# One packed program for three 16-wide attentions, with the clip attention's clamps on GpSimd

## What is computed

```
x = x + tanh(g_xattn[0]) * L0_xattn(layernorm(x), ctx)   # cosine similarity
x = x + tanh(g_ffn[0])   * L0_ffn(layernorm(x))
x = x + tanh(g_xattn[1]) * L1_xattn(layernorm(x), ctx, mask)
x = x + tanh(g_ffn[1])   * L1_ffn(layernorm(x))          # experts
x = x + tanh(g_xattn[2]) * L2_xattn(layernorm(x), ctx)
x = x + tanh(g_ffn[2])   * L2_ffn(layernorm(x))          # experts
x = x + tanh(g_xattn[3]) * L3_xattn(layernorm(x), ctx)
x = x + tanh(g_ffn[3])   * L3_ffn(layernorm(x))
```

```
q = query @ Wq + bq; k = key_value @ Wk + bk; v = key_value @ Wv + bv
attn = softmax(clip(q k^T * scale, -10000, 10000))
x = attn v @ Wo + bo
```

## Time and profile before

| | |
|---|---|
| median of 3 runs | 3416.39 us |
| the runs | 3400.31, 3416.39, 3434.22 us |
| span of the profiled execution | 3390.0 us |
| mean granted clock of TensorE | 0.829 of 2.4 GHz |
| busy: PE, DVE, ACT, POOL | 2575.8, 1580.7, 872.7, 785.2 us |

### The profile page before, as it was taken

One profiled execution on the slowest core, in us unless ns is written; L12 is line 12 of the kernel. 1 busy time (PEld: TensorE's weight loads), 2 busy tenths in 40 slices (PEclk: granted clock), 3 DMA queues, 4 the chain that ended last, 5 costly groups with the idle time before them and its releaser, 6 DMA issues.

```text
span 3390.0 us, 37402 instructions
## 1 busy us (share of the span) xinstructions
PE 2575.8 (76%) x13142; PEld 1918.9 (57%) x13142; DVE 1580.7 (47%) x2934; ACT 872.7 (26%) x2012; POOL 785.2 (23%) x709
## 2 busy tenths in 40 slices
PE   3795885487887728888888577673888884999998
PEld 3574554376666625555556466552555653766665
DVE  3443566256657423333334533224564554454454
ACT  1221342111111103323333112122453451232232
POOL 3103223334334133333434422213000000000000
PEclk8795676699898868888989588786896996988899
DMA  3704441122232230000000013321000000000000
GB/s 115 253 0 57 56 60 54 68 96 98 78 103 91 83 118 5 2 2 2 2 2 0 13 50 95 105 86 55 5 3 2 5 1 0 1 0 0 0 0 25
DMA packets 91147, 151.93 MB, mean 45 GB/s; under 512 B 7612, under 2 KB 75900, under 8 KB 88428
## 3 DMA queue, kind: packets, MB, share of 16 engines
q1 hardware_dynamic: 61820, 101.93, 11.1%
q0 software_dynamic: 8736, 27.76, 2.6%
q10 hardware_dynamic: 20496, 20.97, 1.7%
HBM read 90.51 MB, written 47.19 MB: 41 GB/s over the span
## 4 chain that ended last, share of the span: by engine, by line
PE 57%; issue 20%; DVE 10%; POOL 5%; DMA 3%; ACT 3%; SPq 1%; another core or an unknown queue 1%; ACTq 0%; DVEq 0%; POOLq 0%
PE bank L1898 11%; PE bank L1853 7%; PE bank L1736 6%; PE bank L1915 6%; PE bank L1737 5%; PE bank L1738 5%; PE bank L1939 4%; PE bank L1873 2%; DMA arena<-rows_by_expert 2%; POOL arena L786 2%; DVE nmax L1044 1%; PE bank L1987 1%; DVE split L1332 1%; PE bank L2091 1%; ACT arena L1457 1%
## 5 line engine op out<-in xcount | busy, mean ns | idle before, releaser
L1898 PE MATMUL bank<-arena 64*128 64x256 f32 x1536 | 472.4, 442 | 6.2 <-ACT arena L1457 6.2
L1898 PEld LDWEIGHTS bank<-arena 64*128 64x128 f32 x1536 | 283.0, 207 | 141.6 <-issue 108.5
L1542 ACT ACTIVATE arena<-bank,nmax 128x256 f32<-128x256 f32 x512 | 226.3, 470 | 459.8 <-DVE nmax L1044 457.8
L1915 PE MATMUL bank<-ident,arena 128*128 128x128 f32 x1536 | 272.0, 306 | 74.7 <-POOL arena L829 44.2
L1044 DVE TENSOR_REDUCE nmax<-bank 128x2 f32<-128x512 f32 x256 | 175.8, 690 | 321.0 <-PE bank L1898 316.9
L1457 ACT ACTIVATE arena<-bank 128x512 f32<-128x512 f32 (+1 forms) x346 | 198.2, 580 | 463.1 <-PE bank L1853 112.0
L1736 PE MATMUL bank<-split,ewl 128*128 128x512 f32 x514 | 227.3, 442 | 98.8 <-DVE arena L1329 86.2
L1915 PEld LDWEIGHTS bank<-ident,arena 128*128 128x128 f32 x1536 | 177.6, 151 | 210.1 <-issue 112.2
L700 POOL TENSOR_TENSOR rstd<-rstd,mhalf 128x2 f32<-128x2 f32 x40 | 28.0, 700 | 996.8 <-DVE rstd L972 839.2
L1329 DVE TENSOR_TENSOR arena<-sil,bank 128x512 f32<-128x512 f32 x136 | 93.2, 685 | 315.9 <-ACT sil L1670 300.3
L1737 PE MATMUL bank<-split,ewh 128*128 128x512 f32 x514 | 217.2, 423 | 0.0
(11 more groups left out here) (394 smaller groups left out, 4764.7 us busy)
## 6 DMA issues: line engine op xcount, KB each, us to landing
ew<-in_we SPq DMA_DIRECT2D x32, 768.0 KB, 8.0
ew<-in_we SPq DMA_DIRECT2D x15, 1408.0 KB, 6.1
rows_by_expert<-mrow ACTq DMA_DIRECT2D x1, 20480.0 KB, 58.2
arena<-rows_by_expert SPq DMA_DIRECT2D x23, 512.0 KB, 6.5
rows_by_expert<-arena SPq DMA_DIRECT2D x38, 256.0 KB, 5.4
...
```

The source lines that it names most:

```text
L1542: ins = A(prob[h % 3][:, t * S:(t + 1) * S], src[:, t * S:(t + 1) * S], ACT.Exp, bias=nmax[:, h, t:t + 1], **kw)
L1898: ins = mm(bank[h % 3][:, t * S:(t + 1) * S], q[r0:r0 + 64, gr, t * P:(t + 1) * P], kT[r0:r0 + 64, gr, :], start=True, stop=True)
L1915: ins = tr(bank[3 + k % 2][:, c0:c0 + P], prob[k % 3][:, t * S + kt * P:t * S + (kt + 1) * P], ident[:, :])
```

## The change

L3X and L3F leave the unpacked program and become instances of `Packed` with options: `bias`, `clip`, `proj` (an output product) and `own` (keys and values from x itself, masks by two more rows, registers). The functions `attention` keep L2X alone. All three run the same loops:

- Three rooms (banks 5, 6, 7) instead of two, and one bank for the values. x, queries, keys and values are made for image n+3 and not n+2. Projections are issued in halves, six matmuls at a time; DVE's two output blocks come at heads 5 and 7 and not together at head 8.
- The clip: DVE clamps the maxima (two small instructions) and shifts them by 60, so that exponentials reach at most e^60, and the exponentials are clamped to the range from e^-27 to e^60, in place, 128x512 per head. All 128 of these clamps go to POOL; `by_pool` says how many heads of the first h are POOL's, and DVE's own `clamp` is never issued. PE's `values` wait for the clamps.
- The output product: DVE writes the divided outputs to `on`, PE turns them, ACT copies them to `onT`, PE multiplies by the weights, DVE adds. The output bias times the gate (for L3X with the bias of the values folded in) is added to x by POOL beforehand (`with_bias`).
- For L3F, SP puts the mask rows into `qpack` and `kpack`, 8 DMAs per image; the registers have steps of their own (`register_scores`, `register_turned`, `register_values`, `registers`).
- `kpack` is filled with ones by POOL at the start of L1X and of L3X, where six DMAs did it; the weights of L3X and L3F are split by POOL in L2F.

```diff
+
+
+def by_pool(h):
+
+    return h
...
-        for n in range(-2, B + 1):
-            for what, at in (("xT", n + 2), ("k", n + 2), ("v", n + 2), ("m1", n), ("q", n + 2),
-                             ("z0", n - 1), ("z1", n - 1), ("m0", n + 1)):
-                if 0 <= at < B:
-                    b = sum(self.used) % 2
+        self.place, self.used = {}, [0] * ROOMS
+        for n in range(-3, B + 1):
+            for what, at, here in (("rs", n, own), ("m1", n, True), ("xT", n + 3, True), ("z0", n - 1, True),
+                                   ("rt", n, own), ("z1", n - 1, True), ("rg", n - 1, own), ("q", n + 3, True),
+                                   ("m0", n + 1, True), ("k", n + 3, True), ("ro", n, own), ("w", n - 1, proj),
+                                   ("v", n + 3, True), ("y", n - 1, proj)):
+                if here and 0 <= at < B:
...
+ROOMS = 3
+EXP_HIGH, EXP_LOW = 60.0, -27.0
 L1X = Packed("l1x", 0.25, mask=True)
-L2X = Attn("l2x", 64, 0.125, proj=True, bias=False)
-L3X = Attn("l3x", 16, 0.25, proj=True, bias=True, clip=True)
-L3F = Attn("l3f", 16, 0.25, proj=True, split=True)
+L2X = Attn("l2x", 64, 0.125)
+L3X = Packed("l3x", 0.25, bias=True, clip=True, proj=True)
+L3F = Packed("l3f", 0.25, proj=True, own=True)
 
...
+                for n in range(-3, B):
+                    ahead = 0 <= n + 2 < B
+                    if ahead:
+                        if n >= 1:
+                            sp.wait_ge(m["st"], at["st"] + n * NH)
+                        if n == -2:
+                            sp.wait_ge(m["ones"], at["ones"] + s.total["ones"])
+                            if s.own:
+                                sp.wait_ge(m["mc"], 1)
+                        sp.wait_ge(m["qs"], at["qs"] + 2 * n + 6)
+                        rows_of(qpack[(n + 2) % 3], qhl, 0, (0, 1, 0), m["pq"])
                     if 0 <= n:
...
+                    if not s.own and n + 4 < B:
+                        context(n + 4)
 
             if "l1x" in run:
...
+                def with_bias(n):
+                    pool.wait_ge(g["xn"], entered(s.name, n) * T + T)
+                    if n == 0:
+                        pool.wait_ge(m["bt"], at["bt"] + 1)
+                    rows = x[:, n * T:(n + 1) * T, :]
+                    nc.gpsimd.tensor_tensor(rows, rows, bot[:, :].rearrange("p (o d) -> p o d", o=1).broadcast_to([P, T, D]),
+                                            ALU.add).then_inc(m["xb"], 1)
+
+                def clamp(n, h):
+                    i = n * NH + h
+                    pool.wait_ge(m["e"], at["e"] + i + 1)
+                    w = pT16[i % 8][:, :]
+                    nc.gpsimd.tensor_scalar(w, w, math.exp(EXP_HIGH), math.exp(EXP_LOW), ALU.min, ALU.max)\
+                        .then_inc(m["cl"], 1)
+
...
+                    if ahead and not s.own:
                         context(n + 3)
-                    if n + 3 < B:
-                        root(m, n + 4, rstd[:, :], rstd[:, :], mhalf[:, 0:T])
+                    for h in range(NH):
+                        if s.clip and 0 <= n < B and by_pool(h + 1) > by_pool(h):
+                            clamp(n, h)
+                        if h == 4 and ahead:
+                            filled("xT", n + 3)
+                            parts(xT16, xt[:, :, :], "xs", n + 3)
+                        if h == 9 and ahead:
+                            filled("q", n + 3)
+                            if n + 3 > 0:
+                                pool.wait_ge(m["pq"], at["pq"] + s.loads * (n + 3))
+                            parts(qhl, qf[:, :, :], "qs", n + 3)
+                        if h == 10 and n + 4 < B and not s.own:
+                            root({"asked": asked[s.name]}, n + 5, rstd[:, :], rstd[:, :], mhalf[:, 0:T])
+                        if h == 12 and ahead:
+                            filled("k", n + 3)
+                            if n + 3 > 0:
+                                pool.wait_ge(m["pk"], at["pk"] + s.loads * (n + 3))
+                            parts(khl, kf[:, :, :], "ks", n + 3)
+                        if h == 13 and s.proj and n + 4 < B:
+                            with_bias(n + 4)
 
             def mixture(s):
                 m, r, at = mo, rooms[s.name], s.base
...
+                        ch.link(ts(nmf[:, c, :, :, :], nmf[:, c, :, :, :], -CLAMP / s.qscale, EXP_HIGH / s.qscale,
+                                   ALU.max, ALU.add))
+                        ch.link(ts(nmf[:, c, :, :, :], nmf[:, c, :, :, :], (CLAMP + EXP_LOW) / s.qscale, None, ALU.min))
                     for t in range(T):
...
+                def finish(n):
+                    src, done = made("y", n)
+                    dve.wait_ge(m["xb"], at["xb"] + n + 1)
+                    rows = x[:, n * T:(n + 1) * T, :]
+                    stt(rows, src[:, :].rearrange("p (t d) -> p t d", t=T), gate, rows, ALU.mult, ALU.add).then_inc(done, 1)
...
+                for n in range(-3, B + 2):
                     for h in range(NH):
+                        if h == 0 and s.proj and 0 <= n - 2 < B:
+                            finish(n - 2)
                         if 0 <= n + 1 < B:
                             maximum(n + 1, h)
                             if h == 7:
                                 maxima(n + 1, 0)
                             if h == NH - 1:
                                 maxima(n + 1, 1)
-                        if h == 4 and n + 2 < B:
...
+                        if h == 1 and s.own and 0 <= n < B:
+                            register_maximum(n)
+                        if h in (5, 7) and 0 <= n - 1 < B:
+                            outputs(n - 1, h // 2 - 2)
+                        if h == 8 and s.own and 0 <= n - 1 < B:
+                            with_registers(n - 1)
+                        if h == 9 and s.mask and 0 <= n + 3 < B:
+                            queries(n + 3)
+                        if h == 10 and n + 4 < B and not s.own:
+                            statistics(n + 4)
+                        if h == 12 and s.own and 0 <= n < B:
+                            register_outputs(n)
...
+                def projected(what, n, dst, used, bias):
+                    if n > 0:
+                        act.wait_ge(m[used], at[used] + 2 * n)
+                    src, done = made(what, n)
+                    if s.bias:
+                        for j in range(2):
+                            ins = A(dst[:, j, :], src[:, j * S:(j + 1) * S], ACT.Identity, bias=bias[:, j:j + 1])
...
-                                      lambda t: t[:, :].rearrange("p (t h e) -> p t h e", t=T, h=NH))
...
+                def across(what, n, j, w, of, r):
+                    b, k = s.place[what, n]
+                    if j == 0:
+                        room(what, n)
+                    to = bank[FIRST_ROOM + b]
+                    for c in range(DC):
+                        ins = mm3(to[:, j * S:(j + 1) * S], [t[0:r, c, j * P:(j + 1) * P] for t in w],
+                                  [of[:, u, c, :] for u in range(2)], c == 0, c == DC - 1)
+                    if j == 1:
...
-                    pe.wait_ge(m["e"], s.base["e"] + n * NH + gr * 4 + 4)
+                    pe.wait_ge(m["e"], at["e"] + n * NH + gr * 4 + 4)
+                    if s.clip:
+                        k = by_pool(gr * 4 + 4)
+                        pe.wait_ge(m["cl"], at["cl"] + n * by_pool(NH) + k)
+                        pe.wait_ge(m["cv"], at["cv"] + n * (NH - by_pool(NH)) + gr * 4 + 4 - k)
...
+                def finish(n):
+                    filled("w", n)
+                    to, done = room("y", n)
+                    for t in range(T):
+                        for c in range(DC):
+                            ins = mm(to[:, t * D:(t + 1) * D], onT[:, t * DC + c, :], wo[s.name][:, c, :],
+                                     start=c == 0, stop=c == DC - 1)
+                    ins.then_inc(done, 1)
...
+                for n in range(-3, B + 1):
+                    ahead = 0 <= n + 3 < B
+                    behind = 0 <= n - 1 < B
                     for h in range(NH):
                         heads_of(n, h)
-                        if h == 0 and n + 2 < B:
-                            turned(n + 2)
-                            keys(n + 2)
-                        if h == 1:
-                            if 0 <= n - 1:
-                                values(n - 1, 3)
-                            if n + 2 < B:
-                                values_of(n + 2)
+                        if h == 0 and s.own and 0 <= n < B:
+                            register_scores(n)
+                        if h == 1 and behind:
+                            values(n - 1, 3)
                         if h == 2 and 0 <= n < B:
                             maxima(n, 1)
-                        if h == 3 and n + 2 < B:
-                            queries(n + 2)
+                        if h == 3 and ahead:
+                            turned(n + 3)
```

(20 more changed lines are left out.)

1088 lines of the change are left out of this document (487 added, 601 removed).

## The result

The changed kernel takes 2841.5 us (median of 4 runs, 2833.8 to 2849.8), the one before 3424.3 in the runs beside it: a ratio of 0.832, 95% interval 0.827 to 0.838. That is 8.5 us under the low end of the range (2850), and 97 us under the forecast of 2939. The profiled execution took 2846.9 us, with a span of 2845.1.

The account below looks back on a forecast made before the run. The prediction took L3X and L3F to be bound by TensorE's work. Savings of 40.3 (L1X), 204.6 (L3X) and 232.7 us (L3F), 477.6 in all, took the span from 3390.0 to 2912.4 us, median 2939; range 2850 to 3060.

Parts of the forecast that it names:

- Where the gain comes from: Three 16-wide attentions: L1X 40.3 us less, L3X 204.6, L3F 232.7; other stages within 10 us of now.
- The length of an iteration: Full iterations with projections: 24 us in L1X (from 30.8), 26.5 in L3X, 29.5 in L3F, clock 0.75 to 0.8.
- rival (3): All three stages: TensorE gets the full clock nearly throughout and DVE binds; the low ends, 2843 us; chance 0.08.
- PE's work at the full clock: L1X's full iteration: PE's matmuls and transposes need some 25 us at half clock, some 13 at 2.4 GHz.
- the DVE bound of 20 us: L1X's iteration at full clock: DVE's 16 reductions, its other work and 40 handovers set the pace, 20 us.
- The tail of L1X: L1X's last images: two iterations without projections at 18.6 us each, the last at 13, then 7 of draining.
- cost nothing: L3X's clamps on POOL: value groups' wait just fits, costed at nothing; otherwise some 2 us per image.
- The four subtractions: L3X: DVE's four 8-column subtractions with two SBUF inputs may each wait for a clamp, 2.4 us per image.
- Filling, splits, SP: Filling 57.2, 60 and 55 us; weight splits in L2F cost nothing; SP's 24 DMAs per image, 16 us, hidden.
- The median as span plus 26: Whole kernel: the profiled span lay 26 us under the timed median, so 26 is added to the forecast span.
- All low ends together: Whole kernel: every stage at its low end, 573 us off the 3390 span, plus 26: 2843 us.
- half of a rival: Range's low end, 2850 us: half of the full-clock, DVE-bound case (2843 us, chance 0.08) left out.

Follow-up runs that it names:

- the repetition: The changed kernel run once more with nothing edited, beside a combined variant on the same chip: 2816.5 us, ratio 0.828.

## Why the prediction was right in its direction and too high by 97 us

**Where the gain comes from: right.** All but 7 of 545 us lie in the three stages, and the order of their shares is the one forecast. The other stages moved by 4 us at most.

**The length of an iteration: the step that failed.** "Evener work should cost the clock a little less often than 0.72; I take 24", and with it 26.5 and 29.5. Measured, the five iterations with projections of the three stages are 97.5, 116.5 and 116.5 us long, where 120, 132.5 and 147.5 were forecast: 69.5 us less. The three stages came in 60.7 under; the other terms gave 8.8 back. PE's granted clock was not 0.75 to 0.8: leaving out the first iteration of each stage, it was 1.00 in eleven of the other twelve with projections (0.76 in L3X's second). This was rival (3), which got 0.08; its time, 2843, was met within 2 us. That is luck twice over. Its span of 2817 us is 28 too short (its stages of 211, 232 and 236 us took 221.9, 249.8 and 241.0), and the 26 us that it adds for the median are 30 too long. And its reason was wrong. DVE, expected to be busy for 75% of the time and busy for 91, 85 and 71%, is not the bound at the full clock. In L3F PE is: busy for 23.78 of 23.80 us, and the run with doubled transposed scores shows it by lengthening one for one. For L1X (18.6 of 19.2 us) and L3X (21.0 of 22.3) the busy share says the same; no run tested it.

**PE's work at the full clock: too small.** I put it at some 13 us for L1X, half of 25, with 0.21 us for a pair of score matmuls at the half clock; it is 18.6. The pairs do run beside each other, but their price is that of a long row of them. The timeline of PE in L1X (start us, us, instruction) at 1.00, where two heads stand back to back, where a head stands between other work, and at 0.50:

```profile
416.44 0.28 PE L2037 MATMUL bank<-kpack,qpack 48*128 48x256 f32 x1
416.56 0.28 PE L2051 MATMUL bank<-qpack,kpack 50*128 50x256 f32 x1
...
418.00 0.38 PE L2037 MATMUL bank<-kpack,qpack 48*128 48x256 f32 x1 [0.18 <-DVE nmf L1117]
418.01 0.38 PE L2051 MATMUL bank<-qpack,kpack 50*128 50x256 f32 x1
418.23 0.28 PE L2037 MATMUL bank<-kpack,qpack 48*128 48x256 f32 x1
...
418.44 0.39 PE L2020 MATMUL bank<-ident,nmhl 128*16 128x128 f32 x2
...
435.71 0.58 PE L2037 MATMUL bank<-kpack,qpack 48*128 48x256 f32 x1
...
436.45 0.59 PE L2020 MATMUL bank<-ident,nmhl 128*16 128x128 f32 x2
```

Back to back, the next pair starts after 0.12 us. Between other work a head's two pairs hold PE for 0.44 us (418.00 to 418.44), and for 0.74 at the half clock (435.71 to 436.45). Sixteen heads at 0.44 are 7.0 us, where the sum had 3.5. The six matmuls of half a projection show the same pattern:

```profile
385.95 0.38 PE L1760 MATMUL bank<-xT,wqs 128*128 128x256 f32 x1
386.17 0.28 PE L1761 MATMUL bank<-xT,wqs 128*128 128x256 f32 x1
...
386.64 0.28 PE L1762 MATMUL bank<-xT,wqs 128*128 128x256 f32 x1
386.86 0.39 PE L2037 MATMUL bank<-kpack,qpack 48*128 48x256 f32 x1
```

The first and the last step of a group take 0.22 us, those between 0.12. So in these rows a group costs 0.12 us per matmul or pair and 0.20 more for standing between other work: 0.44 for two pairs, 0.92 for six matmuls. By the starts of its instructions the full iteration at 378.9 us then is 7.0 us of scores, 5.4 of projections (the sum had 3.9), 4.0 of value groups (as in the sum) and 2.4 of turning (1.5), 18.8 in all. The rows of before held a warning: if busy time goes with the clock, PE's 24.4 us at a mean of 0.72 make an estimated 17.6 us at the full clock (24.4 x 0.72), not 13.

So the DVE bound of 20 us that I took as the low end happened to lie near PE's real one, which is why rival (3) fits for another reason. And the 24 came from taking the waits away from L1X's old 30.8 at its old clock, so neither end of it was PE's own time.

**The tail of L1X: wrong the other way.** Forecast 18.6, 18.6, 13; measured 17.0, 22.2, 20.8. The last two images ran at 0.50 throughout, after an iteration in which PE was busy for only 13.5 of 17.0 us. It takes back 9.8 us and is not fixed: the same code had 17.8 and 15.3 in the repetition, after the same iteration (13.6 of 17.4 us busy). What decides between the two stays open.

**The clamps: price right, "cost nothing" wrong.** The clamp in L3X, forecast 0.61, with min, median and max in ns:

```profile
L765 POOL TENSOR_SCALAR pT<-pT x128: 606/614/648, 2337.1 to 2509.3; 128x512 f32<-128x512 f32 x128
```

No wait of PE names it, but with one column in place of 512 the stage is 13 to 22 us shorter. The forecast looked at the full iterations only, where it is 1.2 us, and not at those without projections, where it is 4. The placing itself was the best of the three tried: the Trainium skill (GPSIMD Engine Reference, 4.1 Engine selection) has elementwise work on VectorE, and here L3X with DVE's 0.49 us per clamp is 16 to 26 us longer than with POOL's 0.61. Without the clamps DVE is the fuller engine of the two.

**DVE beside the clamps.** The four subtractions were bounded with 2.4 us per image. In L3X DVE is busy 153.3 us, without the clamps 141.9: 1.4 us per image, 11.4 in all. Of these, 8.7 fall on three small instructions with both ends in SBUF: 6.5 on two that have one input (L1125 and L1127) and 2.2 on the subtractions (L1132). First with clamps, then without, DVE's groups by line:

```profile
L1125 DVE TENSOR_SCALAR nmf<-nmf 128x16 f32<-128x16 f32 x16 | 7.6, 473 | 0.6
L1127 DVE TENSOR_SCALAR nmf<-nmf 128x16 f32<-128x16 f32 x16 | 6.8, 427 | 0.5
L1132 DVE TENSOR_TENSOR nmhl<-nmf,nmhl 128x8 fp32r<-128x8 f32 x32 | 6.1, 232 | 0.5
```

```profile
L1125 DVE TENSOR_SCALAR nmf<-nmf 128x16 f32<-128x16 f32 x16 | 5.1, 322 | 0.5
L1132 DVE TENSOR_TENSOR nmhl<-nmf,nmhl 128x8 fp32r<-128x8 f32 x32 | 3.9, 164 | 0.6
L1127 DVE TENSOR_SCALAR nmf<-nmf 128x16 f32<-128x16 f32 x16 | 2.8, 174 | 0.6
```

The Trainium skill (SBUF — State Buffer, Who interferes with whom) gives the port pair that both engines share as the reason, for instructions with two inputs in SBUF and for `tensor_scalar` in its two-port modes. These rows agree with it in direction for both kinds; that it is the ports, no run here shows.

**Filling, splits, SP: right.** Filling was 56.9, 61.9 and 54.8 us against 57.2, 60 and 55; the ones by POOL, the weight splits in L2F and SP's 24 DMAs per image cost nothing that shows in the stages.

**The median as span plus 26: wrong.** Only 1.8 us lie around the span; before, the profiled execution was simply a short one. That is 30 of the 97 us (2912.4 + 26.6 against 2845.1 - 3.6); the other 67 are the span.

**The range.** All low ends together gave 2843, yet the low end was set at 2850, by leaving out half of a rival. A low end above the sum of the low ends had no row behind it.
